# Edge stages of a relational graph kernel in another order, with gathers held by their ring alone

## The chip, the cores and the metric

The kernel runs on one core of one Trainium2 chip, in one launch. The metric is the device time of that launch in microseconds (us). About 0.2% (7 us) is what a measurement of this kernel can tell from no change.

## The reference, cut to what matters

Two relational graph convolutions over 6250 nodes of 256 values, then a small mixture-of-experts feed-forward block. The two convolutions are where the change lies:

```python
def _mgcn_conv(x, edge_index, edge_type, rel, W_in, W_out, W_loop, b, n):
    src, dst = (edge_index[0], edge_index[1])
    e = edge_index.shape[1]
    half = e // 2
    m = x[src] * rel[edge_type]
    m = jnp.concatenate([m[:half] @ W_in, m[half:] @ W_out], 0)
    deg = jax.ops.segment_sum(jnp.ones((e,), x.dtype), dst, num_segments=n)
    norm = 1.0 / jnp.maximum(deg, 1.0)
    agg = jax.ops.segment_sum(m * norm[dst][:, None], dst, num_segments=n)
    return jnp.tanh(agg + x @ W_loop + b)

h = emb + res * _mgcn_conv(emb, edge_index, edge_type, rel1, ...)
h = h + res * _mgcn_conv(h, edge_index, edge_type, rel2, ...)
return h @ mu_w + mu_b
```

There are 106250 edges, sorted by destination, and 400 relation types. The kernel sums x[src] * rel[type] per destination first and multiplies by the matrices afterwards.

## The kernel before, in words

`build` runs five phases one after the other: `phase_setup` (normalization of x, index tables), `phase_edges` for layer 0, `phase_dense` for layer 0, `phase_edges` for layer 1, then `phase_dense` and `phase_ffn`. The change touches `phase_edges` alone, which runs twice.

In an edge phase the edges come in tiles of 128, four tiles to a group (`GROUP`), 208 groups to a layer. All of a group's work goes through these stages, each a small function of group number g, place q in a ring of four (`GROUPS_IN_RING`) and step i:

- GpSimd (POOL), `gather` (L417 to L430): four indirect DMAs, one per tile, fetch the 128 source rows of 256 values into `xg`, a ring of 16 tiles, so of four groups.
- TensorE (PE), `spread_types` (L592 to L602): one matmul writes each edge's relation type to all 128 partitions of `typ` (two PSUM buffers), and counts `typ_done`.
- ScalarE (ACT), `distance` and `one_hot` (L450 to L463) and VectorE (DVE), `one_hot` (L494 to L501): they make from `typ` the one-hot table `hot` (two buffers), ScalarE two of its four chunks and VectorE two. `distance` waits for `typ_done` of its group and, because it overwrites the table of group g-2, for `rel_done` of g-2. VectorE's `one_hot` waits for both distances of its group.
- PE, `relation_rows` (L604 to L616): 28 matmuls of the table by the relation matrix, split in a high and a low part, give rel[type] for four tiles in `rg` (two PSUM buffers). The last matmul counts `rel_done`; the last of each of the first three tiles counts `rel_tile`.
- DVE, `message` (L503 to L508): `rg` = `xg` * `rg`, after `rel_done` and the gather's landing; it counts `messages`.
- ACT, `high` (L443 to L448) and DVE, `low` (L510 to L515): the product split into `m_hi` and `m_lo`. DVE, `one_window` (L532 to L536): the selection matrix `sel` of the group's window of 64 destinations.
- PE, `one_window` (L619 to L632): eight matmuls sum the group's messages per destination, and count `summed`. ACT, `copy_sums` (L466 to L470): the sums to SBUF. PE, `turn_over` (L634 to L644): two transposes (three in layer 0, where the degrees go along), counting `turned`. DVE, `add_window` (L538 to L547): the sums added into `acc`.

The order of the work on each engine is written out by hand: `over_groups` (L335) takes pairs of a lag and a stage and calls, in every turn k, each stage for group k minus its lag, in the order of the list. The loops are unrolled. Before the change the lists are:

```python
over_groups(pool, (0, gather))
over_groups(act, (0, distance), (2, high), (0, one_hot), (4, copy_sums))
over_groups(dve, (2, message), (1, one_window), (5, add_window), (0, one_hot), (2, low))
over_groups(pe, (0, spread_types), (1, relation_rows), (3, one_window), (4, turn_over))
```

A gather waits for two things: that the message of group g-4 has read the ring's place (`messages`, L422), and, tile by tile, that TensorE has done tile t of the relation rows of group g-2 (`rel_tile` for three tiles, `rel_done` for the last). The waits and counts are semaphores: an engine's instruction counts one up when it completes, and the waiting instruction and all behind it on its engine stand until the value is there. There is a second path for edge lists whose windows are too wide (`long`, `rolled=True`); these inputs don't take it.

## Time and profile before

| | |
|---|---|
| median of 3 runs | 3422.61 us (3421.14 to 3428.74) |
| the profiled execution | 3432.17 us, its span 3430.4 us |
| mean granted TensorE clock of the profiled execution | 0.946 |
| first gather of layer 0 and of layer 1 | 91.6 and 1557.2 us |
| start of the last gather of layer 0 and of layer 1 | 1391.7 and 2844.0 us |
| gathers, messages, relation matmuls | 1664, 416, 11648 |

The profile gives for each engine its busy time and its instructions; the trace behind it gives the start and the duration of each. PE is TensorE's matmuls (their ends are modelled from their size; the starts are recorded), PEld its weight loads, DVE is VectorE, ACT ScalarE, POOL GpSimd. For a gather the POOL row shows the writing of its descriptors, not the landing of its data. A row says in square brackets how long the engine stood idle before the instruction and what the profile takes for the releaser. The name of a releaser is inferred, and "remote" or a DMA of a former phase stands where nothing of this phase fitted.

### The profile page before, as it was taken

To read this page: it belongs to the slowest core of one execution; us is meant where nothing else is said; L and a number is where in the kernel's file an instruction comes from. 1 tells how busy PE (TensorE), PEld (TensorE's weight loads), DVE (VectorE), ACT (ScalarE), POOL (GpSimd) and SP (SyncE) were. 2 spreads that over 40 slices of the span, in tenths; PEclk is the share of its full clock that TensorE was granted. 3 is DMA by queue.
4 is the path that set the end of the run, shared out by engine and by line. 5 is a ranking of instruction groups with operands and counts; after the bars stand their busy time and mean duration, and the time that the engine had idled before them with its cause. 6 is when DMAs were issued, how large, how long until landed. Compare 5 with 4: busy or idle time off the path is not lost. (4 is left out here: it accounts for less than half of the span.)

```text
span 3430.4 us, 61454 instructions
## 1 busy us (share of the span) xinstructions
PE 2915.3 (85%) x21236; PEld 2711.3 (79%) x21236; DVE 2391.5 (70%) x3620; ACT 1852.4 (54%) x3333; POOL 1948.2 (57%) x2028
## 2 busy tenths in 40 slices
PE   3789888888888988697889899888888886776998
PEld 2678878888878888696788888888888876666998
DVE  5677767677776766795666676666676666995666
ACT  5455555555555555584555555555555554444443
POOL 3566666666666656355666666666666664773232
PEclk9999999999999999898999999999999998998999
DMA  7322222222232222243323222332223222332212
GB/s 235 94 85 85 84 85 84 85 85 85 85 86 83 86 83 85 84 158 97 87 85 87 85 87 85 85 87 84 86 85 87 85 85 81 111 112 88 74 64 71
DMA packets 163456, 313.60 MB, mean 91 GB/s; under 512 B 34382, under 2 KB 96270, under 8 KB 163190
## 3 DMA queue, kind: packets, MB, share of 16 engines
q0 software_dynamic: 79872, 218.21, 22.2%
q1 hardware_dynamic: 82389, 91.10, 8.3%
q8 instruction: 153, 2.51, 0.3%
q10 hardware_dynamic: 928, 0.85, 0.1%
q14 instruction: 114, 0.93, 0.1%
HBM read 264.16 MB, written 45.88 MB: 90 GB/s over the span
## 5 line engine op out<-in xcount | busy, mean ns | idle before, releaser
L612 PE MATMUL edge_rg<-edge_rel_hi,edge_hot 128*128 128x256 f32 x6656 | 1574.3, 296 | 50.6 <-issue 41.5
L612 PE MATMUL edge_rg<-edge_rel_lo,edge_hot 128*128 128x256 f32 x4992 | 1347.4, 295 | 32.5 <-issue 31.2
L612 PEld LDWEIGHTS edge_rg<-edge_rel_hi,edge_hot 128*128 128x128 f32 x6656 | 1258.4, 203 | 84.9 <-issue 77.6
L456 ACT ACTIVATE edge_hot<-edge_typ,minus_type 128x512 fp32r<-128x512 f32 x832 | 527.5, 685 | 1164.9 <-remote 382.4
L430 POOL DMA_INDIRECT edge_xg<-emb,src x832 | 799.4, 961 | 509.2 <-issue 228.5
L430 POOL DMA_INDIRECT edge_xg<-h,src x832 | 797.3, 958 | 501.9 <-issue 208.9
L612 PEld LDWEIGHTS edge_rg<-edge_rel_lo,edge_hot 128*128 128x128 f32 x4992 | 1014.7, 203 | 57.9 <-issue 42.6
L508 DVE TENSOR_TENSOR edge_rg<-edge_xg,edge_rg 128x1024 f32<-128x1024 f32 x416 | 510.2, 1226 | 431.2 <-remote 343.7
L499 DVE TENSOR_SCALAR edge_hot<-edge_typ,type_of 128x512 fp32r<-128x512 f32 x832 | 586.0, 747 | 207.0 <-ACT edge_hot L456 174.1
L514 DVE TENSOR_TENSOR edge_m_lo<-edge_rg,edge_m_hi 128x1024 fp32r<-128x1024 f32 x416 | 505.9, 1216 | 2.3 <-ACT edge_m_hi L448 2.3
L462 ACT ACTIVATE edge_hot<-edge_hot 128x512 fp32r<-128x512 f32 x832 | 484.5, 640 | 0.0
L629 PE MATMUL edge_small<-edge_m_hi,edge_sel 128*128 128x258 f32 x1664 | 427.7, 289 | 26.8 <-DVE deg L529 11.9
L448 ACT CAST edge_m_hi<-edge_rg 128x1024 fp32r<-128x1024 f32 x416 | 422.6, 1016 | 10.6 <-DVE edge_rg L508 10.6
L630 PE MATMUL edge_small<-edge_m_lo,edge_sel 128*128 128x256 f32 x1664 | 416.3, 282 | 2.6 <-issue 2.5
L629 PEld LDWEIGHTS edge_small<-edge_m_hi,edge_sel 128*128 128x128 f32 x1664 | 315.7, 190 | 49.2 <-issue 35.3
L630 PEld LDWEIGHTS edge_small<-edge_m_lo,edge_sel 128*128 128x128 f32 x1664 | 315.4, 190 | 1.4 <-issue 1.3
L638 PE MATMUL edge_small<-ident,edge_sums_sb 64*128 64x64 f32 x832 | 142.4, 252 | 192.4 <-ACT edge_hot L462 94.8
L638 PEld LDWEIGHTS edge_small<-ident,edge_sums_sb 64*128 64x128 f32 x832 | 84.6, 141 | 263.0 <-issue 157.1
L601 PE MATMUL edge_typ<-typ,ident_r 104*128 104x512 f32 x416 | 215.4, 519 | 24.8 <-issue 14.0
L525 DVE TENSOR_TENSOR acc<-acc,edge_small 128x128 f32 x416 | 118.5, 285 | 164.4 <-DMA emb_t<-set_e_t 140.9
L519 DVE TENSOR_TENSOR edge_sel<-node_iota,dst_rel 128x256 fp32r<-128x256 f32 x416 | 174.9, 420 | 0.0
L1365 ACT ACTIVATE ffn_work<-ffn_up,ffn_b 128x256 f32<-128x256 f32 x200 | 88.9, 473 | 131.9 <-PE ffn_up L140 130.3
(160 smaller groups left out, 3938.8 us busy)
## 6 DMA issues: line engine op xcount, KB each, us to landing
edge_xg<-emb,src POOLq DMA_INDIRECT x832
edge_xg<-h,src POOLq DMA_INDIRECT x832
set_x_rows<-in_x SPq DMA_DIRECT2D x25, 256.0 KB, 3.6
emb<-set_e_rows SPq DMA_DIRECT2D x25, 256.0 KB, 3.4
emb_t<-set_e_t SPq DMA_DIRECT2D x25, 256.0 KB, 2.9
dense_prev<-emb_t SPq DMA_DIRECT2D x25, 256.0 KB, 2.8
h_t<-dense_work SPq DMA_DIRECT2D x25, 256.0 KB, 2.0
h<-dense_work SPq DMA_DIRECT2D x25, 256.0 KB, 2.1
```

The lines of the kernel that those rows point to most:

```text
L430: pool.indirect_dma_start(xg[:, GROUP * q + t, :], None, nodes, bass.IndirectOffsetOnAxis(ap=at, axis=0)).then_inc(gathered[q], 16)
L448: act.copy(m_hi[:, q % 2, :, 0:DIM], rg[q % 2][:]).then_inc(hi_done, 1)
L456: act.activation(hot[:, q % 2, c], typ[q % 2][:], ACT.Abs, bias=K["minus_type"][:, c:c + 1]).then_inc(distances, 1)
L462: ins = act.activation(hot[:, q % 2, c], hot[:, q % 2, c].bitcast(F32), ACT.Relu, bias=1.0, scale=-1.0)
L499: ins = dve.tensor_scalar(hot[:, q % 2, c], typ[q % 2][:], K["type_of"][:, c:c + 1], None, ALU.is_equal)
L508: dve.tensor_tensor(rg[q % 2][:], xg[:, at, :], rg[q % 2][:], ALU.mult).then_inc(messages, 1)
L514: dve.tensor_tensor(m_lo[:, q % 2], rg[q % 2][:], m_hi[:, q % 2, :, 0:DIM].bitcast(F32), ALU.subtract).then_inc(lo_done, 1)
L601: pe.matmul(typ[q % 2][:], row, K["typ"][0:TYPE_ROWS, q % 2 * GROUP * P:(q % 2 + 1) * GROUP * P], start=True, stop=True).then_inc(typ_done, 1)
L612: ins = pe.matmul(rg[q % 2][:, t, :], hot[:, q % 2, c, t * P:(t + 1) * P], part[:, c, :], start=(c == 0 and part is rel_hi), stop=(c == FULL))
L629: pe.matmul(sums[q % 2][:], lhs, m_hi[:, q % 2, t, :], start=(t == 0), stop=False)
L630: ins = pe.matmul(sums[q % 2][:, 0:DIM], lhs, m_lo[:, q % 2, t, :], start=False, stop=(t == GROUP - 1))
L638: ins = pe.transpose(sums_t[q % 2][:, k, :], sums_sb[:, q % 2, k * P:(k + 1) * P], K["ident"][0:WIN, 0:WIN])
```

## The change

The four lists of stages are changed on three engines; TensorE no longer counts its tiles; and the gather loses its waits for TensorE, so that only `messages` (the ring) holds it.

```diff
--- before.py
+++ after.py
@@ -393,7 +393,6 @@
         distances = s.sem("distances")
         hot_act = s.sem("hot_act")
         rel_done = s.sem("rel_done")
-        rel_tile = s.sem("rel_tile")
         selected = s.sem("selected")
         messages = s.sem("messages")
         hi_done = s.sem("hi_done")
@@ -421,11 +420,6 @@
 
                 wait_past(pool, messages, g + 1 - GROUPS_IN_RING)
                 for t in range(GROUP):
-
-                    if t < GROUP - 1:
-                        wait_past(pool, rel_tile, (GROUP - 1) * (g - 2) + t + 1)
-                    else:
-                        wait_past(pool, rel_done, g - 1)
                     at = K["src"][:, GROUP * g + t:GROUP * g + t + 1]
                     pool.indirect_dma_start(xg[:, GROUP * q + t, :], None, nodes,
                                             bass.IndirectOffsetOnAxis(ap=at, axis=0)).then_inc(gathered[q], 16)
@@ -471,7 +465,7 @@
 
             widest = act.value_load(K["span"][0:1, 0:1], min_val=0, max_val=2 * FAR)
             with act.If(widest < WIN):
-                over_groups(act, (0, distance), (2, high), (0, one_hot), (4, copy_sums))
+                over_groups(act, (0, distance), (2, high), (0, one_hot), (3, copy_sums))
             with act.Else():
                 over_groups(act, (0, distance), (2, high), (0, one_hot), rolled=True)
 
@@ -545,7 +539,7 @@
                         wait_past(dve, deg_added, g)
                     add(q % 2, acc_at - half_at, acc_at, acc_added, deg_added)
 
-                over_groups(dve, (2, message), (1, one_window), (5, add_window), (0, one_hot), (2, low))
+                over_groups(dve, (2, message), (2, one_window), (4, add_window), (2, low), (0, one_hot))
 
             def long():
 
@@ -611,8 +605,6 @@
                         for part in (rel_hi, rel_lo) if c < FULL else (rel_hi,):
                             ins = pe.matmul(rg[q % 2][:, t, :], hot[:, q % 2, c, t * P:(t + 1) * P], part[:, c, :],
                                             start=(c == 0 and part is rel_hi), stop=(c == FULL))
-                    if t < GROUP - 1:
-                        ins.then_inc(rel_tile, 1)
                 ins.then_inc(rel_done, 1)
 
             def short():
@@ -643,7 +635,7 @@
                                            K["ident"][0:WIN, 0:WIN])
                     ins.then_inc(turned, 1)
 
-                over_groups(pe, (0, spread_types), (1, relation_rows), (3, one_window), (4, turn_over))
+                over_groups(pe, (4, one_window), (0, spread_types), (2, relation_rows), (4, turn_over))
 
             def long():
                 def sum_window(q):
```

## Rows read from the trace of the kernel before

**Rows 1.** The page's head and its busy time by engine

```profile
span 3430.4 us, 61454 instructions
PE 2915.3 (85%) x21236; PEld 2711.3 (79%) x21236; DVE 2391.5 (70%) x3620; ACT 1852.4 (54%) x3333; POOL 1948.2 (57%) x2028
```

**Rows 2.** Instructions on tile edge_xg: duration ns min/median/max, first and last start us

```profile
L430 POOL DMA_INDIRECT edge_xg<-emb,src x832: 943/949/1387, 91.6 to 1391.7; - x167
L430 POOL DMA_INDIRECT edge_xg<-h,src x832: 942/949/1190, 1557.2 to 2844.0; - x167
```

**Rows 3.** Busy us per stretch: PE PEld DVE ACT POOL, PE clock, DMA share, GB/s

```profile
600.00:900.00 300.00, 264.34 (x1939) 245.44 (x1937) 212.44 (x336) 166.37 (x288) 184.79 (x194) 0.96 0.30 85
...
1900.00:2200.00 300.00, 266.42 (x1860) 244.82 (x1860) 205.55 (x290) 168.31 (x291) 184.59 (x194) 0.94 0.30 86
```

**Rows 4.** Timeline of PE at 1000 us: start us, us, engine, line, what

```profile
1000.20 0.28 PE L629 MATMUL edge_small<-edge_m_hi,edge_sel 128*128 128x258 f32 x1
...
1001.57 0.50 PE L601 MATMUL edge_typ<-typ,ident_r 104*128 104x512 f32 x1
...
1005.26 0.28 PE L629 MATMUL edge_small<-edge_m_hi,edge_sel 128*128 128x258 f32 x1
...
1007.23 0.34 PE L638 MATMUL edge_small<-ident,edge_sums_sb 64*128 64x64 f32 x2 [0.86 <-issue]
```

**Rows 5.** Timeline of all engines, 2036 to 2042.3 us

```profile
2037.22 1.02 ACT L448 CAST edge_m_hi<-edge_rg 128x1024 fp32r<-128x1024 f32 x1
...
2037.29 1.04 POOL L430 DMA_INDIRECT edge_xg<-h,src  x1 [0.30 <-issue]
...
2037.63 1.41 DVE L499 TENSOR_SCALAR edge_hot<-edge_typ,type_of 128x512 fp32r<-128x512 f32 x2
...
2037.86 0.36 PE L629 MATMUL edge_small<-edge_m_hi,edge_sel 128*128 128x258 f32 x1
...
2038.94 1.22 DVE L514 TENSOR_TENSOR edge_m_lo<-edge_rg,edge_m_hi 128x1024 fp32r<-128x1024 f32 x1
...
2039.86 0.49 PE L601 MATMUL edge_typ<-typ,ident_r 104*128 104x512 f32 x1
...
2039.89 0.94 POOL L430 DMA_INDIRECT edge_xg<-h,src  x1 [0.30 <-issue]
...
2042.01 1.23 DVE L508 TENSOR_TENSOR edge_rg<-edge_xg,edge_rg 128x1024 f32<-128x1024 f32 x1 [1.85 <-remote]
```

**Rows 6.** Timeline of POOL, 2034 to 2056 us

```profile
2036.04 0.95 POOL L430 DMA_INDIRECT edge_xg<-h,src  x1 [1.26 <-PE edge_rg L612]
...
2042.10 0.95 POOL L430 DMA_INDIRECT edge_xg<-h,src  x1 [1.26 <-PE edge_rg L612]
```

**Rows 7.** Timeline of all engines at the end of layer 0's gathers

```profile
1389.19 0.50 PE L601 MATMUL edge_typ<-typ,ident_r 104*128 104x512 f32 x1
...
1391.68 0.99 POOL L430 DMA_INDIRECT edge_xg<-emb,src  x1 [0.31 <-issue]
...
1393.93 0.69 ACT L456 ACTIVATE edge_hot<-edge_typ,minus_type 128x512 fp32r<-128x512 f32 x1 [5.46 <-remote]
...
1394.00 0.29 DVE L525 TENSOR_TENSOR acc<-acc,edge_small 128x128 f32 x1 [2.16 <-DMA emb_t<-set_e_t]
```

**Rows 8.** Timeline of all engines around eight gathers in a row, 1903.8 to 1916.3 us

```profile
1903.86 0.95 POOL L430 DMA_INDIRECT edge_xg<-h,src  x1 [2.37 <-remote]
...
1907.70 0.28 PE L629 MATMUL edge_small<-edge_m_hi,edge_sel 128*128 128x258 f32 x1
...
1909.01 0.50 PE L601 MATMUL edge_typ<-typ,ident_r 104*128 104x512 f32 x1
...
1911.08 1.23 DVE L508 TENSOR_TENSOR edge_rg<-edge_xg,edge_rg 128x1024 f32<-128x1024 f32 x1 [2.67 <-remote]
...
1912.63 0.95 POOL L430 DMA_INDIRECT edge_xg<-h,src  x1 [0.30 <-issue]
...
1915.38 1.27 ACT L456 ACTIVATE edge_hot<-edge_typ,minus_type 128x512 fp32r<-128x512 f32 x2 [7.35 <-DMA dense_prev<-emb_t]
```

## The prediction

> **What bounds the kernel now.** I read the page's busy times first, then the stretches, then the timelines of one turn. No engine is full: PE 85%, DVE 70%, POOL 57% [rows 1]. The stretches show the same in the steady middle of both layers: TensorE 264 and 266 of 300 us busy, all others below 213, at a granted clock of 0.96 and 0.94 [rows 3], so mostly at the higher of its two levels. So I ask what one group costs. The first gather of layer 0 starts at 91.6 and the last at 1391.7, of layer 1 at 1557.2 and 2844.0 [rows 2]; each has 207.75 groups between, so a group takes 6.26 us in layer 0 and 6.19 in layer 1. That is 416 x 6.2 = 2590 of the 3430 us.
>
> What should it take? On TensorE, window sums and transposes take 1001.57 - 1000.20 = 1.37 us, types and relation rows 1005.26 - 1001.57 = 3.69 [rows 4]: 5.06 us without a wait. On POOL a group is four gathers, 1.25 apart where nothing holds them ((1912.63 - 1903.86) / 7) [rows 8], 5.0 us. So 1.2 us of each turn are waits, and in the same view the transposes stand 0.86 us for the copy of their sums [rows 4]: the copy is the last work of ScalarE's turn, and ScalarE began late.
>
> **Why it began late** is the main reading. Window sums follow the relation rows without a gap, so their first matmul at 2037.86 says that a group's relation rows had been issued. VectorE was free from 2038.94 + 1.22 = 2040.16, and yet its message started at 2042.01 [rows 5], 4.15 us after TensorE had finished that group. POOL's next gather starts at 2042.10 after 1.26 idle [rows 6]. Three engines are let go at once, so TensorE's completions are seen late and in a bunch. When? At the end of layer 0 the types were spread at 1389.19, ScalarE and VectorE stood 5.46 and 2.16 us, and both moved at 1393.93 and 1394.00: 1.26 us after the last gather ended (1391.68 + 0.99) [rows 7]. POOL had nothing more to wait for there, so its waits are not what held TensorE's completions; its gathers are. After eight gathers in a row (1903.86 to 1912.63, 1.25 apart) ScalarE moves at 1915.38, 11.52 us after the first [rows 8]; after four (2036.04 [rows 6] to the message at 2042.01 [rows 5]) 5.97 us. So each gather occupies something for (11.52 - 5.97) / 4 = 1.39 us, longer than the 1.25 at which POOL issues it; a long run of gathers builds an arrear, and TensorE's completions wait behind it. Some slip through: in that run of eight the message at 1911.08 came 7.2 us in, 3.4 after its relation rows, while the rest stayed until 1915.38 [rows 8].
>
> The Trainium skill speaks against this reading: "PE and ACT never wait on anyone" (SBUF — State Buffer, Who interferes with whom). It speaks of SBUF ports, and the trace disagrees for completions, by the 1.26 us of [rows 7] against none. By that rule the time would be rival A's.
>
> **The change, part by part.**
>
> 1. *The transposes' stall.* Copies of sums move a turn sooner against the transposes (lag 3 against 4), window sums to the head of TensorE's turn. The copy then has types and relation rows (3.69) to hide behind, and the 0.86 us [rows 4] goes. Late next is the one-hot table.
> 2. *Types a turn sooner, relation rows at lag 2.* ScalarE's distance of group g overwrites the table of g-2, whose relation rows now lie in the same turn, so it starts with the message. From relation rows seen: message 1.23, high part 1.02, low part 1.22, VectorE's one-hot 1.41 [rows 5], 4.88 us with 0.1 for handing over (estimate) 5.0. TensorE wants that table two turns later: from the end of the relation rows a turn's transposes and sums, 1.37, and one whole turn, 5.06, are 6.4 us [rows 4]. So 1.4 us of lateness are covered, more only at TensorE's cost. VectorE's selection and additions lie in its wait for the high part. The chain's 5.0 is under any turn that I expect; no term.
> 3. *Other completions.* Types, sums and transposes now have over 3 us before they are missed; only `rel_done` is urgent. Cost nothing; if they are later than 3 us they join rival B.
> 4. *No `rel_tile`.* Seven completions per group on TensorE become four, 1248 fewer in all. From below: nothing, since the 28 matmuls and the types fill 3.69 at some 0.12 each, counts included. From above: they are heads of the queue that slips through one at a time, so `rel_done` no longer stands behind three. I book it in the share below. The Trainium skill prices a completion at about 26 ns (TensorE: Matmul & The Clock Gate, The cost: per-tile semaphore tail), 1248 of them at 33 us by that estimate.
> 5. *Gathers held by the ring alone.* Four waits per group go from POOL's queue; behind them stood only gathers. Now a gather of g follows the message of g-4 and nothing else; gathers run up to four groups ahead, in runs of four or more at 1.25. Their landing is not at stake, it was in time with two groups ahead. But POOL's pauses were what let completions through, and now only the ring makes them.
> 6. *Fill and drain.* Window sums come one turn later, the addition to acc one sooner in lag (5 to 4). Between 0 and one turn (6 us) a layer; I take 0, because the last stage sits at the smaller lag.
>
> **The sum.** Gathers hold four times 1.39 = 5.55 us of a group, above TensorE's 5.06; that floor stays. A group is *smooth*, 5.55, if `rel_done` slips through during its four gathers. Else two groups' gathers run through, completions come after 11.52, then the message 1.23 and the next gather 0.2 later (estimate): 12.95 for two, 6.48 each. In the rows of eight one of two relation completions slipped through, so I take half and half: 6.02. Gain (6.26 - 6.02 + 6.19 - 6.02) x 208 = 85 us, 3432 - 85 = 3347 for the profiled execution. The runs' median is 9.6 under that execution (3422.6 against 3432.2), so 3337. All smooth: 1.35 x 208 = 281 less, for the median 3141. TensorE's clock I leave at 0.95: its share of waiting hardly moves.
>
> **The rivals.**
>
> A. *TensorE's tiles were the cause.* If completions queue because POOL takes each tile's count, then with `rel_tile` gone they flow, and TensorE's 5.06 bounds: (1.20 + 1.13) x 208 = 485 us less, 2937. The Trainium skill's rule above (SBUF — State Buffer) gives the same. For: the tiles carry three of the seven completions, and POOL waits for each. Against: [rows 7], where sums, types and transposes were late with no tile awaited.
>
> B. *Slower: the pause now ends through VectorE.* Before, the bunch freed POOL itself: 1.26 us idle and on [rows 6]. Now it frees the message first and POOL 1.4 us later, and POOL's runs are longer. If no `rel_done` slips through, every pair of groups takes 12.95: (0.22 + 0.29) x 208 = 106 us more, 3528. It decides below a share of 27% smooth groups (6.48 - 0.27 x 0.93 = 6.23). Worse, if POOL stops after every four: 5.97 + 1.43 = 7.4 a group, 3910. For: gathers in [rows 8] ran unpaced and ScalarE stood 7.35 us. Against: four completions instead of seven, and 1.4 us of cover.
>
> C. *No change.* Turn and arrears balance at 6.2, within 7 us of 3423.
>
> **How the numbers follow.** Forecast 0.48, A 0.12, B 0.32, C 0.08. About 0.2% (7 us) is what a measurement can tell. Forecast and A are faster: 0.60; C same: 0.08; B slower: 0.32. The forecast's own range is 3141 to 3415 (100% down to 27% smooth). The whole range, 3130 to 3530, leaves out A and the worst of B, some 0.18.
>
> **What would show it.** Right: gathers in runs of four at 1.25 with a pause of 0.5 to 1.5 us, no wait of the transposes for their copy, messages starting under 1.5 us after the relation rows in half the turns, a group near 6.0 us. A: messages 0.1 us after the relation rows throughout, group 5.1, POOL hardly idle. B: runs of eight and more, VectorE and ScalarE both idle over 5 us and let go together about 1.3 to 1.8 us after the last gather, TensorE idle before the types. The prediction is wrong if TensorE's completions are prompt while POOL gathers without a pause.

## The result and the profile after

The changed kernel took 3576.84 us (median of four runs, 3575.29 to 3579.3), the kernel before 3421.88 us in the runs beside them: a ratio of 1.0451, 95% interval 1.0439 to 1.0464. It is slower by 155 us. The forecast was 3337 us, and the range ended at 3530, so both missed; rival B had the direction and, as it turns out, most of the mechanism.

That is the answer of one chip. The experiments met seven by number, 11, 7, 3, 10, 15, 14 and 5; the number of the first isn't on record, and it is taken for another chip than 11 because the kernel before took 3395.66 us there, 0.8% less. On six of the seven the kernel before itself takes 2931 to 2934 us, and on the one of these where the changed kernel ran unaltered the change is worth nothing (0.9997, interval 0.9988 to 1.0007). On chip 15 two of thirteen runs of the kernel before, at 3754.62 and 5161.41 us, fell out of line and are left out of the ratios. So there are two results to explain, and the second explains much of the first.

The page of the changed kernel on the first chip begins with the lines that answer to [rows 1]; the groups of instructions below have, after the bar, busy time, mean ns, and the idle time before them with what ended most of it. Lines below the relation rows' wait have moved up by six or eight.

```profile
span 3574.8 us, 61044 instructions
...
PE 2941.7 (82%) x21236; PEld 2721.8 (76%) x21236; DVE 2384.6 (67%) x3620; ACT 1885.2 (53%) x3333; POOL 1924.7 (54%) x2028
...
L606 PE MATMUL edge_rg<-edge_rel_hi,edge_hot 128*128 128x256 f32 x6656 | 1556.3, 293 | 59.0 <-issue 58.1
...
L424 POOL DMA_INDIRECT edge_xg<-emb,src x832 | 787.5, 947 | 587.9 <-DVE edge_rg L502 346.0
L424 POOL DMA_INDIRECT edge_xg<-h,src x832 | 786.7, 946 | 580.1 <-DVE edge_rg L502 345.2
L606 PE MATMUL edge_rg<-edge_rel_lo,edge_hot 128*128 128x256 f32 x4992 | 1340.4, 294 | 85.7 <-issue 82.0
...
L450 ACT ACTIVATE edge_hot<-edge_typ,minus_type 128x512 fp32r<-128x512 f32 x832 | 525.6, 683 | 1030.5 <-remote 888.1
L502 DVE TENSOR_TENSOR edge_rg<-edge_xg,edge_rg 128x1024 f32<-128x1024 f32 x416 | 509.5, 1225 | 738.4 <-remote 676.3
...
L630 PE MATMUL edge_small<-ident,edge_sums_sb 64*128 64x64 f32 x832 | 140.2, 249 | 184.5 <-ACT edge_sums_sb L464 167.1
```

On POOL, VectorE and ScalarE these instructions take what they took within 2%; it is the waits that changed. POOL now stops for VectorE's message (L502) where it stopped for TensorE before [rows 6]. VectorE stands 738 us before its message, 431 in the kernel before, and most of that, 676 us, is ended by what the profile can only call "remote"; so are 888 of the 1031 us before ScalarE's distance, whose whole wait was 1165 us before. Both wait there for TensorE's counts, so "remote" is read here as TensorE's completion seen with no event of TensorE beside it. The mean granted clock is 0.947, against 0.946 before, so the clock is not what differs.

The view of tile edge_xg answers to [rows 2]; its last line is the pauses of the tile's engines that VectorE's message ended, in us and times.

```profile
L424 POOL DMA_INDIRECT edge_xg<-emb,src x832: 940/946/1389, 92.3 to 1459.6; - x167
L424 POOL DMA_INDIRECT edge_xg<-h,src x832: 940/946/1141, 1628.4 to 2982.8; - x167
...
  DVE edge_rg L502: 691.1, 216
```

With 207.75 groups between first and last gather, a group takes 1367.3 / 207.75 = 6.58 us in layer 0 and 1354.4 / 207.75 = 6.52 in layer 1, against 6.26 and 6.19 before. That is (0.324 + 0.325) x 208 = 135 us of the 144.4 by which the two profiled spans differ (3574.8 - 3430.4). Nearly all of the other 10 lie at the seams: from the last gather of layer 0 to the first of layer 1 168.8 us against 165.5, from the last gather to the end 592.0 against 586.4. The 216 pauses come to one in every 1.93 groups, 3.20 us each. In layer 1 the shape is regular: nearly everywhere eight gathers, which are two groups, and one pause, 13.08 us together. In layer 0 74 such cycles of 13.18 us are mixed with 48 runs of four gathers. Twenty of these take 5.80 us with their pause, but 21 take 7.51, and all 48 come to 6.63 on average, no less than half a long cycle.

One cycle of layer 1, on the timeline of all engines (start us, us, engine, line, what, and in brackets the idle time before it and its releaser), cut to a few rows of each engine:

```profile
2293.59 0.94 POOL L424 DMA_INDIRECT edge_xg<-h,src  x1 [3.43 <-DVE edge_rg L502]
...
2294.84 0.94 POOL L424 DMA_INDIRECT edge_xg<-h,src  x1 [0.30 <-issue]
...
2295.72 0.34 PE L630 MATMUL edge_small<-ident,edge_sums_sb 64*128 64x64 f32 x2 [1.18 <-ACT edge_sums_sb L464]
...
2296.86 1.22 DVE L502 TENSOR_TENSOR edge_rg<-edge_xg,edge_rg 128x1024 f32<-128x1024 f32 x1
...
2300.57 0.28 PE L606 MATMUL edge_rg<-edge_rel_hi,edge_hot 128*128 128x256 f32 x1
...
2300.78 0.34 PE L630 MATMUL edge_small<-ident,edge_sums_sb 64*128 64x64 f32 x2
...
2302.33 0.95 POOL L424 DMA_INDIRECT edge_xg<-h,src  x1 [0.30 <-issue]
...
2302.87 0.38 PE L606 MATMUL edge_rg<-edge_rel_hi,edge_hot 128*128 128x256 f32 x1
...
2304.27 0.28 PE L606 MATMUL edge_rg<-edge_rel_lo,edge_hot 128*128 128x256 f32 x1 [1.02 <-issue]
...
2305.18 1.27 ACT L450 ACTIVATE edge_hot<-edge_typ,minus_type 128x512 fp32r<-128x512 f32 x2 [4.74 <-remote]
...
2305.19 1.23 DVE L502 TENSOR_TENSOR edge_rg<-edge_xg,edge_rg 128x1024 f32<-128x1024 f32 x1 [3.48 <-remote]
...
2306.69 0.94 POOL L424 DMA_INDIRECT edge_xg<-h,src  x1 [3.41 <-DVE edge_rg L502]
```

Eight gathers go out 1.25 us apart, from 2293.59 to 2302.33. A group's relation rows end at 2300.57 + 0.28 = 2300.85, and the transposes behind them start at once, but VectorE takes them up at 2305.19, 4.34 us later and 1.91 after the last gather ended. ScalarE is let go in the same moment, and its distance waits for no gather, so it isn't the landing of the fetched rows that VectorE waited for. Then the message takes 1.23 us, and 0.27 later POOL begins the next run of eight. The cycle is 11.60 + 1.23 + 0.27 = 13.10 us for two groups.

### The profile page after: what moved, and what is told of

It reads as the page before. It is cut to its first block and busy times, and to the rows that moved or that the text cites. A ratio compares the mean times of both kernels' runs of the same rounds, so it can differ in the third digit from the quotient of the medians.

```text
span 3574.8 us, 61044 instructions
## 1 busy us (share of the span) xinstructions
PE 2941.7 (82%) x21236; PEld 2721.8 (76%) x21236; DVE 2384.6 (67%) x3620; ACT 1885.2 (53%) x3333; POOL 1924.7 (54%) x2028
## 5 line engine op out<-in xcount | busy, mean ns | idle before, releaser
L606 PE MATMUL edge_rg<-edge_rel_hi,edge_hot 128*128 128x256 f32 x6656 | 1556.3, 293 | 59.0 <-issue 58.1
L606 PE MATMUL edge_rg<-edge_rel_lo,edge_hot 128*128 128x256 f32 x4992 | 1340.4, 294 | 85.7 <-issue 82.0
L606 PEld LDWEIGHTS edge_rg<-edge_rel_hi,edge_hot 128*128 128x128 f32 x6656 | 1242.7, 201 | 105.1 <-issue 103.3
L424 POOL DMA_INDIRECT edge_xg<-emb,src x832 | 787.5, 947 | 587.9 <-DVE edge_rg L502 346.0
L424 POOL DMA_INDIRECT edge_xg<-h,src x832 | 786.7, 946 | 580.1 <-DVE edge_rg L502 345.2
L606 PEld LDWEIGHTS edge_rg<-edge_rel_lo,edge_hot 128*128 128x128 f32 x4992 | 1001.9, 201 | 123.2 <-issue 104.8
L502 DVE TENSOR_TENSOR edge_rg<-edge_xg,edge_rg 128x1024 f32<-128x1024 f32 x416 | 509.5, 1225 | 738.4 <-remote 676.3
L621 PE MATMUL edge_small<-edge_m_hi,edge_sel 128*128 128x258 f32 x1664 | 475.7, 314 | 40.0 <-issue 29.4
L622 PE MATMUL edge_small<-edge_m_lo,edge_sel 128*128 128x256 f32 x1664 | 434.3, 289 | 35.1 <-issue 34.9
L622 PEld LDWEIGHTS edge_small<-edge_m_lo,edge_sel 128*128 128x128 f32 x1664 | 323.9, 195 | 44.2 <-issue 43.7
L630 PE MATMUL edge_small<-ident,edge_sums_sb 64*128 64x64 f32 x832 | 140.2, 249 | 184.5 <-ACT edge_sums_sb L464 167.1
L595 PE MATMUL edge_typ<-typ,ident_r 104*128 104x512 f32 x416 | 181.7, 438 | 48.5 <-issue 32.7
L464 ACT COPY edge_sums_sb<-edge_small 64x258 f32<-64x258 f32 x416 | 147.8, 355 | 52.5 <-DMA emb_t<-set_e_t 47.0
```

What stands on the lines that cost most here:

```text
L424: pool.indirect_dma_start(xg[:, GROUP * q + t, :], None, nodes, bass.IndirectOffsetOnAxis(ap=at, axis=0)).then_inc(gathered[q], 16)
L502: dve.tensor_tensor(rg[q % 2][:], xg[:, at, :], rg[q % 2][:], ALU.mult).then_inc(messages, 1)
L595: pe.matmul(typ[q % 2][:], row, K["typ"][0:TYPE_ROWS, q % 2 * GROUP * P:(q % 2 + 1) * GROUP * P], start=True, stop=True).then_inc(typ_done, 1)
L606: ins = pe.matmul(rg[q % 2][:, t, :], hot[:, q % 2, c, t * P:(t + 1) * P], part[:, c, :], start=(c == 0 and part is rel_hi), stop=(c == FULL))
L621: pe.matmul(sums[q % 2][:], lhs, m_hi[:, q % 2, t, :], start=(t == 0), stop=False)
L622: ins = pe.matmul(sums[q % 2][:, 0:DIM], lhs, m_lo[:, q % 2, t, :], start=False, stop=(t == GROUP - 1))
```

## The experiments

Each expectation names the theories that it tells apart; in short they are these. **Theory 1:** gathers hold up the reports of TensorE's completions, each for some 1.4 us, and the holds add up when gathers follow one another faster; the ring lets them run longer, so the change costs by its gathers. **Theory 2:** nothing is held; the new order of the stages, or the ring's wait through VectorE by itself, makes the cycle. Two more were forced by the results: **theory C**, that it depends on the chip whether gathers hold anything, and **theory D**, that the change is slower whatever the chip.

The first four ran on one chip (number 11), where the kernel before took 3395.66 us (median of 13 runs).

### The order alone

Only the three lists of stages are changed; gathers still wait for TensorE's tiles.

```diff
 kernel before
-(0, distance), (2, high), (0, one_hot), (4, copy_sums)
+(0, distance), (2, high), (0, one_hot), (3, copy_sums)
-(2, message), (1, one_window), (5, add_window), (0, one_hot), (2, low)
+(2, message), (2, one_window), (4, add_window), (2, low), (0, one_hot)
-(0, spread_types), (1, relation_rows), (3, one_window), (4, turn_over)
+(4, one_window), (0, spread_types), (2, relation_rows), (4, turn_over)
```

> Kernel: the new order of stages on ScalarE, VectorE and TensorE, with the gathers still held by TensorE's tiles and relation rows as before. Theory 1 (the gathers: each occupies about 1.4 us of what TensorE's completions must pass, while POOL issues one every 1.25 us, so long runs of gathers hold the completions back): POOL is again let go by TensorE itself, runs of eight without a pause become rare, and the time falls to the kernel before or below it, 3300 to 3425 us. Theory 2 (the order: ScalarE's distance now waits for relation rows of its own turn, and that is what costs): the time stays near the changed kernel, 3550 to 3600 us.

Measured: 3402.80 us, ratio 1.0019 (1.0007 to 1.0031). The gathers' first and last starts, on tile edge_xg:

```profile
L430 POOL DMA_INDIRECT edge_xg<-emb,src x832: 943/949/1295, 93.0 to 1380.4; - x167
L430 POOL DMA_INDIRECT edge_xg<-h,src x832: 943/949/1193, 1540.7 to 2815.7; - x167
```

A group takes 6.20 and 6.14 us. The order alone is worth next to nothing here: its 0.19% is at the edge of what a measurement can tell. The time is what theory 1 expected, but one of its signs missed. Runs of eight gathers did not become rare: there are 66 of them against 10 in the kernel before (on the first chip), each with its pause 12.3 us, so 6.2 a group. A run of eight costs no more than the rest as long as TensorE itself ends the pause.

### The ring alone

The gathers of the changed kernel, the order of the kernel before.

```diff
 kernel before
-                    if t < GROUP - 1:
-                        wait_past(pool, rel_tile, (GROUP - 1) * (g - 2) + t + 1)
-                    else:
-                        wait_past(pool, rel_done, g - 1)
...
-                    if t < GROUP - 1:
-                        ins.then_inc(rel_tile, 1)
```

> Kernel: the order of stages of the kernel before, with the gathers held by their ring alone and TensorE's tiles not counted. Theory 1: unpaced gathers run eight and more in a row and TensorE's completions come after them, 3480 to 3620 us. Theory 2: the order is the old one, so the time is that of the kernel before, 3410 to 3435 us.

Measured: 3523.87 us, ratio 1.0393 (1.0369 to 1.0417). POOL's timeline has the same runs of eight as the changed kernel:

```profile
2036.26 0.95 POOL L424 DMA_INDIRECT edge_xg<-h,src  x1 [3.32 <-DVE edge_rg L502]
2037.51 0.94 POOL L424 DMA_INDIRECT edge_xg<-h,src  x1 [0.30 <-issue]
...
2044.99 0.94 POOL L424 DMA_INDIRECT edge_xg<-h,src  x1 [0.30 <-issue]
2049.18 0.94 POOL L424 DMA_INDIRECT edge_xg<-h,src  x1 [3.25 <-DVE edge_rg L502]
```

The cycle is 12.92 us here. So the gathers' part carries nearly all of the loss, 3.9 of the 4.5% that were measured on the first chip, and the cycle comes without the new order. This edit takes away the waits and the counts of TensorE's tiles together; neither was tried by itself.

### A pause between gathers, too short

The changed kernel, with GpSimd writing a small spare tile behind every gather and waiting for its own write before the next.

```diff
 changed kernel, behind each gather
+                    wait_past(pool, paused, GROUP * g + t)
+                    pool.memset(spare[:], 0.0).then_inc(paused, 1)
```

> Kernel: the changed kernel, and POOL clears a small spare tile after each gather, which makes the gathers start further apart than 1.25 us. Theory 1: if they start 1.43 us or more apart no arrear builds, messages start within 0.5 us of the end of the relation rows, a group takes 5.7 to 6.0 us and the kernel 3230 to 3350 us. Theory 2: POOL's pace is not what holds TensorE's completions, and the time stays at 3577 us or grows.

Measured: 3545.39 us, ratio 1.0443 (1.0425 to 1.0460). The write went into the 0.30 us that POOL idles between gathers anyway:

```profile
2080.54 0.95 POOL L426 DMA_INDIRECT edge_xg<-h,src  x1 [2.89 <-DVE edge_rg L506]
2081.49 0.17 POOL L429 MEMSET edge_spare<- 128x64 f32 x1
2081.82 0.95 POOL L426 DMA_INDIRECT edge_xg<-h,src  x1 [0.16 <-issue]
```

Gathers were 1.28 us apart in place of 1.25. As a test of spacing this is a miss: it changed the spacing by 0.03 us, to less than 1.39, and nothing follows from it for or against theory 1. It does bound the order's share: new order, ring and writes together cost 4.4% on the chip where the ring alone cost 3.9.

### Half of the gathers

From the fifth group on two gathers a group in place of four. The products of the other two tiles use the rows that the first groups left, so this part of the sums is left out; all other work is as in the changed kernel.

```diff
 changed kernel
-                for t in range(GROUP):
+                for t in range(GROUP if g < GROUPS_IN_RING else GROUP // 2):
...
-                dve.wait_ge(gathered[q], 16 * GROUP * (i + 1))
+                dve.wait_ge(gathered[q], 16 * GROUP + 8 * GROUP * i)
```

> Kernel: the changed kernel with only two of the four gathers of each group from the fifth group on (half of the source rows are not fetched, their messages use stale rows). Theory 1: two gathers occupy 2.8 us of a group of 5.06, the completions are prompt, a group takes 5.05 to 5.3 us and the kernel 2950 to 3060 us. Theory 2: gathers are not what the turn waits for, 3550 to 3600 us.

Measured: 2948.16 us in one run, 0.868 of the kernel before on that chip. A group takes 5.0 us, and TensorE is busy without a gap in the middle of a layer, as the stretch 500 to 800 us shows (columns as in [rows 3]):

```profile
500.00:800.00 300.00, 300.00 (x2376) 285.57 (x2375) 262.61 (x415) 212.95 (x358) 112.85 (x120) 1.00 0.19 53
```

The page's groups for the relation rows and the message:

```profile
L606 PE MATMUL edge_rg<-edge_rel_hi,edge_hot 128*128 128x256 f32 x6656 | 1467.6, 283 | 1.7 <-issue 1.7
...
L502 DVE TENSOR_TENSOR edge_rg<-edge_xg,edge_rg 128x1024 f32<-128x1024 f32 x416 | 511.3, 1229 | 94.5 <-PE edge_rg L606 67.5
```

This is the strongest evidence for theory 1. No wait was taken from TensorE, no completion dropped and no order changed, and VectorE's idle time before the message fell from the changed kernel's 738 us to 95 (on different chips of that kind), TensorE's idle time before the matmuls of its relation rows from 145 (59.0 + 85.7) to 2. Two gathers of 1.39 us hold 2.8 of 5.0 us; four hold 5.6, more than TensorE needs.

It is one run, and one could ask whether the chip held anything at all while it ran. The head of the same execution answers that, because there the first four groups still fetch all their tiles and 18 gathers go out without a pause:

```profile
110.52 0.28 PE L606 MATMUL edge_rg<-edge_rel_hi,edge_hot 128*128 128x256 f32 x1
...
113.92 0.95 POOL L424 DMA_INDIRECT edge_xg<-emb,src  x1 [0.30 <-issue]
...
117.56 1.23 DVE L502 TENSOR_TENSOR edge_rg<-edge_xg,edge_rg 128x1024 f32<-128x1024 f32 x1 [3.08 <-remote]
...
123.74 1.23 DVE L502 TENSOR_TENSOR edge_rg<-edge_xg,edge_rg 128x1024 f32<-128x1024 f32 x1 [1.32 <-PE edge_rg L606]
```

The relation rows that end at 110.80 are seen at 117.56, 6.76 us late and 2.69 after the last of the 18 gathers ended. The next group's rows end at 123.63, behind that run, and are seen at once, at 123.74; so it stays, with a median of 0.11 us over both layers. Long runs hold completions on this chip in this run, and pairs of gathers with pauses of 2.8 us don't. Whether the smaller number or the pause does it is not separated.

### Four kernels on a chip where nothing is held

The next four were meant to take the hold apart: the gathers' distance, the length of their runs, their bytes, and three gathers in place of four. In the last two part of the gathered values is not fetched, so they leave out part of the sums.

```diff
 f1: changed kernel, behind each gather (a group is 6 writes)
+                    for n in ((0, 1) if t % 2 == 0 else (2,)):
+                        wait_past(pool, paused, GROUP // 2 * 3 * g + t // 2 * 3 + n)
+                        pool.memset(spare[:], 0.0).then_inc(paused, 1)
 f2: changed kernel, ahead of a group's first gather
+                wait_past(pool, rel_done, g - 1)
 e6: changed kernel, from the fifth group on 64 values an edge
+        quarters = nodes.rearrange("n (a d) -> (n a) d", a=4)
...
-                    pool.indirect_dma_start(xg[:, GROUP * q + t, :], None, nodes,
+                    wide, rows = (DIM, nodes) if g < GROUPS_IN_RING else (64, quarters)
+                    pool.indirect_dma_start(xg[:, GROUP * q + t, 0:wide], None, rows,
 f4: changed kernel, from the fifth group on three gathers
-                for t in range(GROUP):
+                for t in range(GROUP if g < GROUPS_IN_RING else GROUP - 1):
...
-                dve.wait_ge(gathered[q], 16 * GROUP * (i + 1))
+                dve.wait_ge(gathered[q], 16 * GROUP + 16 * (GROUP - 1) * i)
```

The spacing:

> The changed kernel, with GpSimd writing a spare tile between gathers, once after every second gather and twice after the others (the single write took 0.17 us and left gathers 1.28 us apart in the earlier run; a second one behind it should add 0.33, so 1.28 and 1.61 us in turn, 1.45 on average). Theory 1 (gathers less than about 1.4 us apart hold up the reports of TensorE's completions, and the hold adds up over a run of them): no arrear builds, so VectorE's products come at even distances, the two-group cycle of 13.1 us is gone and a group takes what GpSimd needs, 4 x 1.45 = 5.8 us or a little more; 5.8 to 6.1 us a group, ratio to the kernel before 0.94 to 0.99. Theory 2 (the cycle is made by the wait on VectorE alone, and spacing has no part in it): GpSimd has more work in every group and can't run ahead as fast, a group stays at 6.5 us or more, ratio 1.04 to 1.08.

One wait a group:

> The changed kernel, whose four gathers of a group wait once, ahead of the first, for TensorE's relation rows of two groups back; no completion of a single tile is counted. Theory 1: gathers go out in fours at 1.25 us, behind a completion that is itself seen late; runs of four hold up less than runs of eight, but every group has one: about 4 x 1.39 us after the release, so 6.0 to 6.4 us a group, ratio 0.98 to 1.02. Theory 2 (what costs is that gathers may run two groups ahead): the limit of two groups is back, so the time is that of the order alone, 1.00 within 0.5%.

A quarter of the bytes:

> The changed kernel, whose gathers fetch from the fifth group on 64 values in place of 256 for each edge (as many descriptors, a quarter of the bytes); the other three quarters of each row in the products are those of the first four groups, so this part of the sums is left out. If what holds up TensorE's reports is the bytes that the gathers move, a group falls to 5.0 to 5.3 us, as with half of the gathers (5.03), and the time to about 2950 to 3070 us against 3577. If it is the descriptors or GpSimd's issue, which are unchanged, the runs of eight at 1.25 us and the pause of 3.4 us stay, and the time stays within 1.5% of the changed kernel's.

Three gathers:

> The changed kernel with three gathers a group in place of four from the fifth group on; the fourth tile's rows are those of the first four groups, so this part is left out. Theory 1 (each gather holds the reports for about 1.4 us, and they come through once the sum is worked off): 3 x 1.39 = 4.2 us is less than TensorE's 5.06, so arrears don't last from one group to the next, though runs of three or six still delay some; 5.1 to 5.7 us a group, time 2960 to 3230 us. Theory 2 (the share of late groups does not depend on the number of gathers): 6.0 us or more a group, over 3350 us.

Measured, on chip 7, where **the kernel before took 2931.24 us** (median of 13 runs) and not 3400: f1 3196.18 us, ratio 1.0906 (1.0888 to 1.0924); f2 2935.60, 1.0014 (1.0004 to 1.0024); e6 2934.45 and f4 2936.88, one run each. Three very different loads of gathers come to the same time, because the hold that they were to vary isn't there. f4's gathers came in threes, 1.25 us apart with 1.54 of pause, f2's ran 1.25 apart with hardly a pause, and both left TensorE busy for all of the 300 us from 500 to 800. Neither the bytes nor the number of gathers was tested by this, since the time can't fall below TensorE's own work. The spacing (f1) made GpSimd the bound: the second write added 0.2 us, VectorE stood 332 us for gathers to land, and a group took (1275.1 - 91.1) / 207.75 = 5.70 us:

```profile
L426 POOL DMA_INDIRECT edge_xg<-emb,src x832: 950/952/1295, 91.1 to 1275.1; - x167
```

### The changed kernel again, on a third chip

Theory C had to be tried with nothing altered.

> The changed kernel itself, nothing altered. On the chip of the last four runs the kernel before took 2931.24 us, where it had taken 3421.88 and 3395.66 on the two others, and gathers 1.25 us apart went with TensorE's products never late. Theory C (chips differ in whether gathers hold up the reports of TensorE's completions, and the change only costs where they do): if the kernel before takes about 2930 us here, the changed kernel is within 0.5% of it (a group of 5.0 us, TensorE's own); if it takes about 3400 us, the ratio is 1.04 to 1.05 as before, with pauses of 3.4 us after eight gathers. Theory D (the change is slower whatever the chip): 1.04 or more in both cases.

> The changed kernel with one or two writes of the spare tile between gathers, as run before (there gathers ended 1.28 and 1.47 us apart in turn, a group took 5.67 and 5.71 us, all of it GpSimd's, and the ratio was 1.0906 to a kernel before of 2931.24 us). On a chip where the kernel before takes about 3400 us: Theory 1 (the hold adds up only if gathers come closer than about 1.4 us) gives 5.7 to 6.1 us a group and a ratio of 0.93 to 0.99; if the hold doesn't depend on the distance, 6.5 us or more, 1.04 or more. On a chip where it takes about 2930 us: 1.09 again.

Measured on chip 3, where the kernel before took 2934.44 us: the changed kernel 2934.52, ratio 0.9997 (0.9988 to 1.0007); the paced one 1.0907 (1.0889 to 1.0925). That is theory C's number, and theory D is out. The page of the same program there begins so:

```profile
span 2933.2 us, 61044 instructions
...
PE 2719.8 (93%) x21236; PEld 2592.0 (88%) x21236; DVE 2398.1 (82%) x3620; ACT 1897.9 (65%) x3333; POOL 1936.4 (66%) x2028
...
L606 PE MATMUL edge_rg<-edge_rel_hi,edge_hot 128*128 128x256 f32 x6656 | 1464.7, 283 | 0.0
...
L424 POOL DMA_INDIRECT edge_xg<-h,src x832 | 787.2, 946 | 264.6 <-issue 253.2
L450 ACT ACTIVATE edge_hot<-edge_typ,minus_type 128x512 fp32r<-128x512 f32 x832 | 526.8, 684 | 612.7 <-PE edge_rg L606 591.0
...
L502 DVE TENSOR_TENSOR edge_rg<-edge_xg,edge_rg 128x1024 f32<-128x1024 f32 x416 | 511.2, 1229 | 79.3 <-PE edge_rg L606 62.1
```

Its tile edge_xg:

```profile
L424 POOL DMA_INDIRECT edge_xg<-emb,src x832: 942/946/1295, 91.7 to 1142.1; - x167
L424 POOL DMA_INDIRECT edge_xg<-h,src x832: 942/946/1146, 1305.7 to 2345.1; - x167
```

And its stretch 500 to 800 us:

```profile
500.00:800.00 300.00, 300.00 (x2375) 285.38 (x2374) 262.67 (x416) 212.13 (x356) 227.81 (x238) 1.00 0.36 105
```

GpSimd's gathers take 946 ns in the median on both chips, ScalarE's and VectorE's instructions in the lines shown agree within 4 ns. What is gone are the waits for "remote", which no longer lead on any of these lines: the message stood 738 us in the edge stages there and 79 here, and TensorE's idle time before the matmuls of its relation rows went from 145 us to none. A group takes 5.06 and 5.00 us, TensorE's own work, and the two layers together (1.52 + 1.52) x 208 = 632 of the 642 us between 3576.84 and 2934.52. The stretch is that of half the gathers on chip 11, each engine's busy time within 1 us, save POOL's and the DMAs' columns.

The head of layer 0 shows the difference most plainly. On both chips the first sixteen gathers go out without a pause. On the first chip the relation rows of the first group end at 108.17 and the message starts at 115.56, 7.39 us later; on chip 3 they end at 107.65 and it starts at 107.77, 0.12 us later. The two messages, first chip and chip 3:

```profile
115.56 1.23 DVE L502 TENSOR_TENSOR edge_rg<-edge_xg,edge_rg 128x1024 f32<-128x1024 f32 x1 [11.02 <-PE edge_rg L606]
...
107.77 1.23 DVE L502 TENSOR_TENSOR edge_rg<-edge_xg,edge_rg 128x1024 f32<-128x1024 f32 x1 [3.59 <-PE edge_rg L606]
```

The timeline of all engines shows it at one place further on:

```profile
2038.82 0.95 POOL L424 DMA_INDIRECT edge_xg<-h,src  x1 [0.30 <-issue]
...
2040.07 0.95 POOL L424 DMA_INDIRECT edge_xg<-h,src  x1 [0.30 <-issue]
2040.10 0.28 PE L606 MATMUL edge_rg<-edge_rel_hi,edge_hot 128*128 128x256 f32 x1
...
2040.31 0.34 PE L630 MATMUL edge_small<-ident,edge_sums_sb 64*128 64x64 f32 x2
...
2040.49 1.23 DVE L502 TENSOR_TENSOR edge_rg<-edge_xg,edge_rg 128x1024 f32<-128x1024 f32 x1 [0.15 <-PE edge_rg L606]
```

The relation rows end at 2040.38 and the message starts at 2040.49, 0.1 us later, in the midst of gathers 1.25 us apart that never pause.

### One wait a group, and the spacing, on four more chips

The edits of f2 and f1 ran on four more chips, since on one of the first kind they would have told whether the loss comes from gathers running two groups ahead, and whether the hold depends on their distance.

> The changed kernel with one wait a group for TensorE's relation rows of two groups back, ahead of the first gather. On a chip where the kernel before takes about 2930 us it is within 0.5% of it, as in the run before. On one where it takes about 3400 us: if the gathers' running two groups ahead of TensorE is what costs there (runs of eight, then a pause), the ratio is 1.00 to 1.02 with gathers in runs of four; if losing the counts of single tiles costs as well, runs of four released by a late completion give 6.4 us a group or more, 1.02 to 1.05.

> The changed kernel with one or two writes of the spare tile between gathers. On a chip where the kernel before takes about 2930 us: 1.09 again. On one where it takes about 3400 us: Theory 1 (the hold adds up only if gathers come closer than about 1.4 us) gives 5.7 to 6.1 us a group and a ratio of 0.93 to 0.99; if the hold doesn't depend on the distance, 6.5 us or more, 1.04 or more.

> The changed kernel with one wait a group for TensorE's relation rows of two groups back, sent again in the hope of a chip where the kernel before takes about 3400 us (three of the five so far took about 2930 us, where it is at 1.00). There: if the gathers' running two groups ahead of TensorE is what costs (runs of eight, then a pause), the ratio is 1.00 to 1.02 with gathers in runs of four; if losing the counts of single tiles costs as well, 6.4 us a group or more, 1.02 to 1.05. On a chip of 2930 us: 1.00 again.

> The changed kernel with one or two writes of the spare tile between gathers, sent again in the hope of a chip where the kernel before takes about 3400 us. There Theory 1 (the hold adds up only if gathers come closer than about 1.4 us) gives 5.7 to 6.1 us a group and a ratio of 0.93 to 0.99; if the hold doesn't depend on the distance, 6.5 us or more, 1.04 or more. On a chip of 2930 us: 1.09 again.

> As k1: the changed kernel with one wait a group for TensorE's relation rows of two groups back. On a chip where the kernel before takes about 3400 us: if the gathers' running two groups ahead is what costs, 1.00 to 1.02; if losing the counts of single tiles costs as well, 1.02 to 1.05. On a chip of 2930 us: 1.00 again.

> As k2: the changed kernel with writes of a spare tile between gathers. On a chip where the kernel before takes about 3400 us: 0.93 to 0.99 and 5.7 to 6.1 us a group if the hold adds up only where gathers come closer than about 1.4 us, 1.04 or more if it doesn't depend on their distance. On a chip of 2930 us: 1.09 again.

> As m1, the last try for a chip where the kernel before takes about 3400 us: the changed kernel with one wait a group for TensorE's relation rows of two groups back. There 1.00 to 1.02 if the gathers' running two groups ahead is what costs, 1.02 to 1.05 if losing the counts of single tiles costs as well. On a chip of 2930 us: 1.00 again.

> As m2: the changed kernel with writes of a spare tile between gathers. On a chip where the kernel before takes about 3400 us: 0.93 to 0.99 if the hold adds up only where gathers come closer than about 1.4 us, 1.04 or more if it doesn't depend on their distance. On a chip of 2930 us: 1.09 again.

| chip | before, us | one wait a group: ratio | spaced: ratio |
|---|---|---|---|
| 10 | 2930.69 | 1.0017 (1.0007 to 1.0027) | 1.0917 (1.0899 to 1.0935) |
| 15 | 2930.57 | 1.0018 (1.0007 to 1.0028) | 1.0903 (1.0883 to 1.0922) |
| 14 | 2934.34 | 1.0011 (1.0002 to 1.0021) | 1.0909 (1.0891 to 1.0927) |
| 5 | 2930.89 | 1.0020 (1.0011 to 1.0030) | 1.0914 (1.0896 to 1.0932) |

All four were of the second kind. They agree, on four more chips, with nothing being held there, and leave the two questions about the first kind unanswered. One small thing: one wait a group reads 0.1 to 0.2% slower on all five chips where it ran, which the changed kernel without it does not on chip 3. That is at the edge of what a measurement can tell, and why was not followed up.

## Why the prediction was wrong

**The mechanism on the chip that was predicted for was right.** TensorE's completions are seen late behind runs of gathers. The 1.39 us that a gather holds, worked out from [rows 8] and [rows 5], carries over. The message that ends a run of eight comes 11.60 us after the first gather, against 11.52; in layer 0, behind runs of four with the long pause, it comes 7.51 - 1.23 - 0.27 = 6.01 us after it, against 5.97; and (11.60 - 6.01) / 4 is 1.40. Half of the gathers, which removes half of that hold, removes nearly all of the waiting.

**The step that failed is the sum's share of smooth groups, half of them at 5.55 us.** The prediction read in [rows 8] that one of two relation completions slips through during eight gathers, and took from it that half of the groups would cost 5.55 us. The rows did not show that. POOL's next gather after that run, which the prediction did not use, is this one:

```profile
1916.20 0.95 POOL L430 DMA_INDIRECT edge_xg<-h,src  x1 [2.63 <-remote]
```

So those eight gathers, with the one completion in their midst, took 1916.20 - 1903.86 = 12.34 us, 6.17 for each of the two groups, and neither was smooth. The changed kernel has the same pattern. In the cycle shown above, the message at 2296.86 is the one that comes through in time: it is why POOL goes on from the fourth gather to the fifth. The one at 2305.19 is late and ends the pause. A completion in the middle is part of the cycle of two groups and saves nothing. What the change added is how the pause ends. By count that gather is the first of layer 1's group 58. It waits for the message of group 54, which had been made from 1904.00 on, and for TensorE's first tile of group 56, whose seven matmuls run from 1909.35 to 1910.34. So in [rows 8] TensorE's late count ended the pause, and in the changed kernel it is the message behind a late count, as rival B says.

What the runs showed in place of one half: no smooth group in layer 1, and in layer 0 20 of 208 near 5.80 us, paid back by 21 near 7.51, which is the worse case of rival B (7.4). With no smooth groups the prediction's own formula gives 12.95 us for two groups, 6.48 each, and 3528 us. Measured were 6.58 and 6.52, 0.07 more on average; the cycle shown has 0.08 more up to the message and 0.07 more up to the next gather. The mechanism was booked under rival B at 0.32, and the range, which ended at 3530, was too short above by 47 us.

Point by point, by the numbers of the prediction:

1. *The transposes' stall* did not go. Before the transposes of the changed kernel TensorE stands 184.5 us, 167.1 of them for the copies of sums; in the cycle shown it is 1.18 us. In the kernel before it was this line:

```profile
L638 PE MATMUL edge_small<-ident,edge_sums_sb 64*128 64x64 f32 x832 | 142.4, 252 | 192.4 <-ACT edge_hot L462 94.8
```

   The copy has a turn more of lag, but it is still the last of ScalarE's turn, and that turn begins when a late completion lets it. Where nothing is late (chip 3) the same transposes wait 3.4 us in all.
2. *Types sooner, relation rows at lag 2*: no term was booked, and with the order alone at 1.0019 none is seen.
3. *Other completions*: likewise, no term and none seen.
4. *No `rel_tile`.* The upper bound, that fewer completions in the queue would let `rel_done` through, did not come true: with them gone, in the old order, the pause of POOL is 3.3 us, as in the changed kernel. The Trainium skill's price for a completion (TensorE: Matmul & The Clock Gate, The cost: per-tile semaphore tail) would have made 1248 of them worth 33 us, as an estimate. The runs speak against it for this kernel: on chip 3, where TensorE is full, the kernels with and without them differ by -0.12 to +0.07%, at most 3.5 us. The two kernels differ in the order of the stages too, whose share wasn't measured on such a chip.
5. *Gathers held by the ring alone* is where the loss is: 1.0393 by itself. The prediction had the reason in its text (POOL's pauses let completions through, and now only the ring makes them) and then priced it by the share of smooth groups. What the per-tile waits did was to stop the gathers for 1.26 us often [rows 6]; the ring stops them for 3.4 us every second group.
6. *Fill and drain* was taken as 0 of 0 to 6 us a layer; the stretches behind the last gathers grew by 3.3 and 5.6, other work included.

Two slips of the text move nothing: 416 x 6.2 is 2579, and the 2590 there is by the unrounded 6.23; and three lists of stages change, not four.

**Rival A** said that without the tiles' counts TensorE's 5.06 us would bound, for 2937 us. As a theory of the change it is out, since on chip 11 the counts went and the lateness stayed. As a number it is what chips of the second kind give, 2934.52, though there the kernel before gives it too, with its counts. The Trainium skill's rule that "PE and ACT never wait on anyone" (SBUF — State Buffer, Who interferes with whom) was said to be contradicted by [rows 7]. It is, on chips of the first kind, as far as it is taken to cover completions; on those of the second kind the trace agrees with it, at 0.1 us from the relation rows to the message under gathers without a pause. The prediction had named exactly this, prompt completions while POOL gathers without a pause, as what would prove it wrong. There it came true, and it proves one tacit assumption wrong: that what gathers hold is a property of the program.

**What stays open.** What differs between the kinds of chip is not known. Of the first kind were the chip of the result, at 3421.88 us, and chip 11; of the second chips 7, 3, 10, 15, 14 and 5. No chip was seen as both, but the two of the first kind came first in time and all six of the second kind after them. So it is not shown that the chip is the cause: something that changed between the two sets, in time or in what else ran beside the kernel, would look the same. Whether the hold goes by descriptors, bytes or GpSimd's issue, whether gathers 1.45 us apart would avoid it, and whether one wait a group would give the 4.5% back on the first kind, was tried on the second kind only. The order's own share beside the ring was not measured cleanly on one chip (1.0451 on the first chip for both; on chip 11 1.0393 for the ring, 1.0443 for both with the writes).

No version with all its work beats the kernel before. On the second kind TensorE is busy all the time in the edge stages, so there only less work on TensorE could make them shorter; on the first kind the time between 3400 and 2930 us is there to be won, and none of these edits wins it.

## What to carry to other kernels

A wait that seems to be in the way may be what paces a queue: before taking it out, ask what the queue will do in the time that it gains, and price the longest run that it can then make, not the average. When a trace shows a pattern once (eight gathers, one message in the middle, a pause), check whether it is the whole cycle of a rival before splitting it into shares. And before explaining a wait that no instruction accounts for, run the kernel on a second chip: here 460 to 490 us of 3400 come and go with the chip, three times what the change does. The per-tile waits are worth keeping: on one kind of chip the kernels with and without them take the same time, and on the other the waits save 4%.

## What the hardware showed that was not expected

- Two kinds of chip for the same program: 3396 and 3422 us on two, 2931 to 2934 on six, with the changed kernel's instructions on ScalarE, VectorE and GpSimd of equal length within 1.3%. Chip and time of the run are not separated.
- On the first kind TensorE's completions are seen late behind gathers 1.25 us apart: 4.3 us in the cycle shown, and 7.4 us behind the sixteen at the head of layer 0. With pauses of 2.8 us after every second gather they are prompt, at 0.11 us.
- There TensorE not only reports late but also stops, inside a row of 28 matmuls with no wait between them in the program: 1.02 us at 2304.27 in the cycle shown, 145 us of idle time before them in all, against 0.0 on the second kind. Whether late reports or late instructions are the cause of both was not separated.
- On the second kind 832 gathers in a row, 1.25 us apart through a whole layer, delay nothing: the median from the end of the relation rows to the message is 0.11 us.
